# Score matmuls of the dot attention in two 128x64 tiles, and its softmax denominators dealt out anew

## What is computed

```python
# layer 0
x_l = (x @ W + b).reshape(N, 8, 64)
scores = alpha_l[:, None, :] * alpha_r[None, :, :]        # per head, N x N
att = softmax(where(adj > 0, scores, -9e15), axis=1)
x = layernorm(x + relu(einsum('ijh,jhc->ihc', att, x_l)))
# layer 1: "dot attention"
q = x (as 8 heads of 64) * 64 ** -0.5; k = x2; v
scores = einsum('hnd,hmd->hnm', q, k)                     # per head, N x N
attn = softmax(where(adj > 0, scores, -9e15), axis=-1)
x = layernorm(x + einsum('hnm,hmd->hnd', attn, v))
```

## Time and profile before

| | |
|---|---|
| median of 3 runs | 4104.07 us (4103.87 to 4105.66) |
| profiled execution, its own time | 4103.82 us |
| its span, first to last instruction | 4102.3 us |
| mean granted TensorE clock, share of 2.4 GHz | 0.950 |
| busy share of the span: PE, DVE, ACT, POOL | 94%, 76%, 62%, 37% |
| dot attention | from about 2009 to 3940 us |

### The profile page before, as it was taken

How to read it: one execution, slowest core, us unless ns; L and a number is a source line. 1 busy time by engine, 2 the same in 40 slices (tenths; PEclk the granted TensorE clock), 3 DMA queues, 4 the chain that set the end, 5 groups by cost and what they waited for, 6 DMA issues and landing times. The chain is left out here.

```text
span 4102.3 us, 55678 instructions
## 1 busy us (share of the span) xinstructions
PE 3871.6 (94%) x19385; PEld 1354.5 (33%) x19385; DVE 3128.7 (76%) x3078; ACT 2527.7 (62%) x2396; POOL 1525.1 (37%) x1115
## 2 busy tenths in 40 slices
PE   7887999999999999976699999999999999999987
PEld 5564222222222222235333333333333333333345
DVE  5555999999999999978677677676777676677656
ACT  3444888888888888842255555555555555555520
POOL 3332000000000000015467666666766666676620
PEclk9998999999999999975799999999999999999975
DMA  7875111111111111136699999999999999999864
GB/s 272 295 275 181 39 40 40 49 45 40 41 39 39 52 44 39 41 118 233 160 183 185 191 190 192 190 190 184 185 190 192 190 190 188 186 184 192 179 170 144
DMA packets 339912, 592.36 MB, mean 144 GB/s; under 512 B 29248, under 2 KB 201280, under 8 KB 339776
## 3 DMA queue, kind: packets, MB, share of 16 engines
q0 software_dynamic: 84224, 302.29, 37.5%
q1 hardware_dynamic: 238400, 262.89, 21.2%
q10 hardware_dynamic: 17152, 25.43, 1.8%
HBM read 262.70 MB, written 59.38 MB: 79 GB/s over the span
## 5 line engine op out<-in xcount | busy, mean ns | idle before, releaser
L1117 DVE TENSOR_TENSOR a_weights<-a_psS,maskT 128x1024 f32<-128x1024 f32 x1024 | 1205.6, 1219 | 582.1 <-ACT a_psS L1082 582.1
L1082 ACT ACTIVATE a_psS<-a_psS,a_shift 128x1024 f32<-128x1024 f32 x1024 | 1071.7, 1084 | 801.3 <-PE a_psS L1010 801.2
L477 ACT ACTIVATE g_weights<-al_bc,g_shift,g_xl 128x1024 f32<-128x1024 f32 x1024 | 1187.8, 1232 | 166.7 <-DVE g_total L523 80.4
L516 DVE TENSOR_TENSOR g_weights<-g_weights,maskT 128x1024 f32<-128x1024 f32 x1024 | 1175.6, 1218 | 97.5 <-ACT g_weights L477 96.6
L1010 PE MATMUL a_psS<-a_q,a_k 128*128 128x512 f16 x4096 | 974.5, 381 | 18.0 <-DMA a_k<-k_scratch 16.6
L1027 PE MATMUL a_psO<-a_weights,a_v 128*64 128x512 f32 x4096 | 988.0, 604 | 0.0
L568 PE MATMUL g_psO<-g_weights,g_xl 128*64 128x512 f32 x4096 | 965.9, 603 | 17.8 <-DVE g_weights L516 17.8
L1140 POOL TENSOR_TENSOR a_pool_total<-a_pool_total,a_weights 128x1024 f32<-128x1024 f32 x336 | 898.5, 2674 | 0.0
L1010 PEld LDWEIGHTS a_psS<-a_q,a_k 128*128 128x128 f16 x4096 | 358.7, 98 | 798.5 <-DVE a_weights L1117 312.5
L1148 POOL DMA_DIRECT2D a_dma_total<-a_weights x480 | 415.9, 867 | 523.7 <-DVE a_weights L1117 415.3
L599 POOL DMA_DIRECT2D o_scratch<-g_o x16 | 8.9, 559 | 1387.9 <-ACT g_d L486 1387.9
(11 more groups left out here) (135 smaller groups left out, 1846.9 us busy)
## 6 DMA issues: line engine op xcount, KB each, us to landing
a_dma_total<-a_weights POOLq DMA_DIRECT2D x512, 512.0 KB, 5.1
adj_sb<-in_adj_dram SPq DMA_DIRECT2D x128, 512.0 KB, 5.5
g_xl<-xl_scratch SPq DMA_DIRECT2D x128, 260.0 KB, 2.8
a_k<-k_scratch SPq DMA_DIRECT2D x256, 128.0 KB, 5.1
a_v<-in_L_gnn_v_dram SPq DMA_DIRECT2D x128, 256.0 KB, 3.1
al_bc<-alpha_scratch SPq DMA_DIRECT2D x16, 1024.0 KB, 4.9
f_oT<-o_scratch SPq DMA_DIRECT2D x16, 1024.0 KB
a_q<-q_scratch SPq DMA_DIRECT2D x64, 256.0 KB, 6.9
```

The lines of the kernel that those rows point to most:

```text
L477: nc.scalar.activation(w[:, u % NP, h, :], al_bc[:, par, h, :], ACT.Exp, bias=shift_bc[:, par, h:h + 1], scale=xl[:, slot, u % KB, 2 * C + ...
L516: nc.vector.tensor_tensor(w[:, u % NP, h, :], w[:, u % NP, h, :], maskT[:, ds(q * JB + u, 1), ds(ic * IC, IC)] .rearrange("p a c -> p (a c)"),
L1082: nc.scalar.activation(psS[n % RING][:], psS[n % RING][:], ACT.Exp, bias=shift_bc[:, g % 2, h:h + 1], scale=SCALE).then_inc(exped, 1)
L1117: nc.vector.tensor_tensor(w[:, u % NP, h, :], psS[n % RING][:].rearrange("p a c -> p (a c)"), maskT[:, j, (g // PAIRS) * IC:(g // PAIRS + ...
```

## The change

Three things are altered in `attend_dot`.

1. Each score matmul of 128 keys becomes two of 64 keys. The first has keys 0 to 63 of the tile as stationary operand (128x64) and writes partitions 0 to 63 of the same `psS` bank, the second has keys 64 to 127 and writes partitions 64 to 127. The moving operand of both is the same. A unit has 16 score matmuls instead of 8.
2. The elementwise sums are dealt out anew. Head 0: GpSimd adds all 32 tiles (31 additions in a group instead of 22). Head 1: VectorE takes tiles 2, 3, 7, 11, ... 31 (9 tiles, 8 additions, as many as it made for head 0 before), and transfers take the other 23, alternating between the two chains by their place among these (`dma_place`), not by `j`. The waits follow.
3. `denominators` has the same 8 calls in another order: two for head 0 (`pool_total`), then six for head 1 (both transfer totals, `dve_total`).

```diff
--- before.py
+++ after.py
@@ -928,18 +928,27 @@
 
         block = ctx.enter_context(nc.Block())
 
-        def by_pool(j):
-
-            return j == 1 or j >= 4 and j % 4 != 3
-
         def pool_adds_by(u):
 
             g, j = divmod(u, NT)
-            return g * sum(by_pool(t) for t in range(NT)) + sum(by_pool(t) for t in range(j + 1))
+            return g * (NT - 1) + j
+
+        def by_dve(j):
+
+            return j == 2 or j % 4 == 3
 
         def dve_adds_by(u):
 
             return (u + 1) // 4
+
+        def dma_place(j):
+
+            return sum(not by_dve(t) for t in range(j))
+
+        def dma_adds_by(u):
+
+            g, j = divmod(u, NT)
+            return g * len(range(dma_place(j) % 2, dma_place(NT), 2)) + dma_place(j) // 2 + 1
 
         @block.sync
         def _(sp):
@@ -1007,10 +1016,12 @@
                         pe.wait_ge(masked, n - RING + 1)
                     for hf in range(2):
                         for part in range(2):
-                            last = nc.tensor.matmul(psS[n % RING][:, hf, :],
-                                                    k_sb[:, slot, h, (u % KB) * P:(u % KB + 1) * P],
-                                                    q_sb[:, par, part, h, hf * HALF:(hf + 1) * HALF],
-                                                    start=(part == 0), stop=(part == 1))
+                            for low in (0, C):
+                                keys = (u % KB) * P + low
+                                last = nc.tensor.matmul(psS[n % RING][low:low + C, hf, :],
+                                                        k_sb[:, slot, h, keys:keys + C],
+                                                        q_sb[:, par, part, h, hf * HALF:(hf + 1) * HALF],
+                                                        start=(part == 0), stop=(part == 1))
                     last.then_inc(scored, 1)
 
             def values(u):
@@ -1033,16 +1044,16 @@
                 pe.wait_ge(o_taken, g + 1)
                 pe.wait_ge(pool_added, pool_adds_by((g + 1) * NT - 1))
                 pe.wait_ge(dve_added, dve_adds_by((g + 1) * NT - 1))
-                for chain in range(2):
-                    pe.wait_ge(dma_added[chain], 16 * (g + 1) * (NT // 2))
-                for step, totals in enumerate(((pool_total[:], dma_total[:, g % 2, 0, :]),
-                                               (dve_total[:], dma_total[:, g % 2, 1, :]))):
-                    for h in range(2):
-                        for hf in range(2):
-                            row = 32 * (2 * h + hf)
-                            last = nc.tensor.matmul(psO[row:row + 32, 0, :], onesF[:, 0:32],
-                                                    totals[h][:, hf * HALF:(hf + 1) * HALF],
-                                                    start=(step == 0), stop=(step == 1))
+                for j in (NT - 3, NT - 2):
+                    pe.wait_ge(dma_added[dma_place(j) % 2], 16 * dma_adds_by(g * NT + j))
+                for h, total, first, close in ((0, pool_total[:], True, True),
+                                               (1, dma_total[:, g % 2, 0, :], True, False),
+                                               (1, dma_total[:, g % 2, 1, :], False, False),
+                                               (1, dve_total[:], False, True)):
+                    for hf in range(2):
+                        row = 32 * (2 * h + hf)
+                        last = nc.tensor.matmul(psO[row:row + 32, 0, :], onesF[:, 0:32],
+                                                total[:, hf * HALF:(hf + 1) * HALF], start=first, stop=close)
                 last.then_inc(d_summed, 1)
 
             for u in range(GROUPS * NT):
@@ -1092,15 +1103,15 @@
         def _(dve):
             def add(u):
                 g, j = divmod(u, NT)
-                dve.wait_ge(masked, 2 * u + 1)
+                dve.wait_ge(masked, 2 * u + 2)
                 if j == 3:
                     if g > 0:
                         dve.wait_ge(d_summed, g)
-                    other = w[:, (u - 1) % NP, 0, :]
+                    other = w[:, (u - 1) % NP, 1, :]
                 else:
                     dve.wait_ge(dve_added, dve_adds_by(u - 1))
                     other = dve_total[:]
-                nc.vector.tensor_tensor(dve_total[:], other, w[:, u % NP, 0, :], ALU.add).then_inc(dve_added, 1)
+                nc.vector.tensor_tensor(dve_total[:], other, w[:, u % NP, 1, :], ALU.add).then_inc(dve_added, 1)
 
             def mask(u, h):
                 g, j = divmod(u, NT)
@@ -1111,9 +1122,10 @@
                     dve.wait_ge(w_used, freed + 1)
                     if h == 0:
                         dve.wait_ge(pool_added, pool_adds_by(freed + 1 if freed % NT == 0 else freed))
+                    elif by_dve(freed % NT):
                         dve.wait_ge(dve_added, dve_adds_by(freed + 1 if freed % NT == 2 else freed))
                     else:
-                        dve.wait_ge(dma_added[freed % 2], 16 * (freed // 2 + 1))
+                        dve.wait_ge(dma_added[dma_place(freed % NT) % 2], 16 * dma_adds_by(freed))
                 nc.vector.tensor_tensor(w[:, u % NP, h, :], psS[n % RING][:].rearrange("p a c -> p (a c)"),
                                         maskT[:, j, (g // PAIRS) * IC:(g // PAIRS + 1) * IC],
                                         ALU.mult).then_inc(masked, 1)
@@ -1141,22 +1153,23 @@
 
             def add_by_dma(u):
                 g, j = divmod(u, NT)
-                chain = u % 2
+                chain = dma_place(j) % 2
+                before = dma_adds_by(u) - 1
                 pool.wait_ge(masked, 2 * u + 2)
-                if j >= 2:
-                    pool.wait_ge(dma_added[chain], 16 * (u // 2))
+                if before > 0:
+                    pool.wait_ge(dma_added[chain], 16 * before)
+                if dma_place(j) >= 2:
                     pool.dma_start(dma_total[:, g % 2, chain, :], w[:, u % NP, 1, :], accum_op=ALU.add
                                    ).then_inc(dma_added[chain], 16)
                 else:
-                    if u >= 2:
-                        pool.wait_ge(dma_added[chain], 16 * (u // 2))
                     if g >= 2:
                         pool.wait_ge(d_summed, g - 1)
                     pool.dma_start(dma_total[:, g % 2, chain, :], w[:, u % NP, 1, :]).then_inc(dma_added[chain], 16)
 
             for u in range(GROUPS * NT):
-                add_by_dma(u)
-                if by_pool(u % NT):
+                if not by_dve(u % NT):
+                    add_by_dma(u)
+                if u % NT > 0:
                     add(u)
 
 
```

## The result

| | before | after |
|---|---|---|
| median | 4104.86 us (4103.87 to 4106.24, 4 runs) | 3990.85 us (3988.95 to 3992.29, 4 runs) |
| profiled execution, its own time | 4103.82 us | 3992.29 us |
| its span | 4102.3 us | 3990.8 us |
| mean granted TensorE clock | 0.950 | 0.948 |

The ratio is 0.9722, 95% interval 0.9705 to 0.9739: 2.8% faster, 114 us by the medians. The forecast was 3990 us, range 3983 to 4014.

A forecast was written before the change was run, and what follows sets the result against it. TensorE was taken to set the dot stage's time. Savings of 105.6 us in 15 groups, 7.7 in the first and 0.2 at the end sum to 113.5, from 4103.8 to 3990 us, range 3983 to 4014.

The forecast's parts named there:

- TensorE bounds, and only its stream counts: Dot stage: TensorE, busy for all of its 1790.00 us, sets the time, so only its stream's cost matters.
- 0.24 to 0.255 us of each period is the passage, paid for width: Dot stage: switching between scores and values costs 0.24 us per 3.70 us unit; equal widths bring 3.445, 0.255 less.
- the first spacing after a passage: Score block: the first gap between matmuls after a switch from values may be long, the others nearer to 0.216 us.
- Halves keep the price of the whole: Score block: 16 matmuls of 64 columns cost what 8 of 128 did, 0 extra; at the other bound 1.74 us more.
- The two rows taken as nearest: Trace evidence for the split scores: layer 0's 32-wide rounds, 0.054 us an instruction, and 128-column loads, at most 0.12 each.
- The middle case in R1: Score halves overlap only partly, as three tiles gave 2.38 times: 0.27 us a pair, time near 4220 us; no separate chance.
- R1: Score matmuls: the two halves do not stream together; fully apart about 4880 us; chance 0.09.
- Denominators 0.86 dearer a group: Group border: head 1's two tiles get three calls each, 6 rounds for 4, 2.58 us, 0.86 more on TensorE.
- A group 113.06 us: Dot stage: 32 units of 3.445 us plus 2.58 and 0.24 at the border make 113.06 us, 120.1 before.
- The verdict: GpSimd in the dot stage: its 31 additions, 93 us (bounds 81 and 105), stay covered in a group of 113.
- one term: GpSimd: an addition without a transfer was taken as 3.0 us from start to start, bounds 2.62 and 3.39.
- Fewer transfers bring nothing: Dot stage: nothing on TensorE waits for a transfer until the very end, where 1.1 us less wait nets 0.2 us.

The follow-up runs named there:

- split_only: The kernel before with only the score matmuls split into two halves of 64 keys, sums and denominators as before: 3977.24 us, ratio 0.9688.
- deal_only: The changed kernel with the score split undone, so new sums and denominator order with 128-wide scores: 4114.99 us, ratio 1.0026.
- one_tile: The changed kernel with both halves of every score matmul sent to one column tile, half of the scores left out: 4869.43 us.
- fold_chain: The changed kernel with VectorE adding one of the two transfer totals to its own, leaving head 1 four denominator calls instead of six: 3977.07 us.
- no_vector_adds: The changed kernel without VectorE's additions: GpSimd adds all 32 tiles of head 0, transfers take all 32 of head 1: 3978.26 us.
- head1_wide: The changed kernel with head 1's scores 128 wide again, head 0's still in two halves of 64: 4117.8 us.
- unit_apart: The changed kernel with a unit's score matmuls reordered: keys 0 to 63 of both heads, then keys 64 to 127 of both: 4052.62 us.
- halves_apart: The changed kernel with, for each head, the four score matmuls of keys 0 to 63 before the four of keys 64 to 127: 3991.67 us.

## Why the prediction was right, point by point

**TensorE bounds, and only its stream counts.** Right: `split_only`, `deal_only`, `one_tile`, `fold_chain` and `no_vector_adds` moved by what their streams of rounds and passages say (3978, 4117, 4870, 3977, 3977 expected; 3977, 4115, 4869, 3977, 3978 measured), although, between 2140 and 3780 us, GpSimd's load was between 0.55 and 0.89 of the stretch and the DMA share between 0.49 and 0.98 (`one_tile` the lowest, `no_vector_adds` the highest).

**0.24 to 0.255 us of each period is the passage, paid for width.** Right in size, 3.44 instead of 3.70. The trace of before already had the evidence in two places, each difference alone, and `head1_wide` confirms it with the kernel's own matmuls. What I had only guessed, that the first spacing after a passage is the long one, is right, but it is a small part for the scores: in the trace of before the first of the seven spacings is 0.226, the others 0.216; the values' first round is 0.05 longer than the others. The larger part, 0.10 and 0.09, lies between the last round of one kind and the first start of the next.

**Halves keep the price of the whole.** Right (16 records span 1.89); `one_tile` shows the 880 us that hung on it. The load of 64 columns takes 0.110 us (median), that of 128 columns took 0.098 before, so per column the loads did become slower, and they stay hidden. The two rows taken as nearest, the 32-wide rounds and the loads in a row, were good guides. The middle case in R1, from three tiles at 2.38 times (the Trainium skill, TensorE: Matmul & The Clock Gate, "Measured speedup vs the span model"), did not come true: two tiles gave the full two. Three tiles occur in no run here.

**Denominators 0.86 dearer a group.** Right: 2.72 for 1.85, and 12.1, 13.6 and 13.8 us by `deal_only`, `split_only` and `fold_chain`.

**A group 113.06 us.** Measured 113.02. In the profiled pair the dot stage, from its first scores to the last copy of denominators, is 1927.95 and 1813.87 us long, 114.1 less for 113.5 forecast. By parts: 8.1 up to the first denominators for 7.7, and 105.9 for 105.8 in the fifteen groups behind them and the end. It begins 2.5 us later than in the profile of before, for which nothing in the change speaks; in the profiles of the eleven kernels it begins anywhere from 2010.2 to 2015.1. So the mechanism and its terms are confirmed to about half a microsecond, but that the total came within 1 us of the median is partly luck.

**GpSimd.** The verdict was right, one term was mis-sized: an addition with no transfer issued beside it is 2.35 us long and starts 2.80 after the one ahead (2901.05 to 2903.85), not 3.0; the one right behind the issue of a transfer is 2.65. The prediction said that no such addition occurs before; the first additions of the 16 groups are of that kind there, and 2.35 us long (2346 to 2358 ns). The margin was a little larger than forecast. `no_vector_adds` shows the other end: with a transfer in every unit additions in the stretch read start 2.9 to 3.3 us apart, which still fits under 3.445.

**Fewer transfers bring nothing.** Right, and the runs go further than the text did: the new deal as a whole brings nothing either. I had costed its 0.86 us at the border without noting that the split with the old deal would be the faster kernel.

## What to carry to other kernels

Where TensorE alternates between matmuls whose stationary operands have different widths, compare a block between passages with the same block in a row: what is over (here 0.255 us in 3.70) comes back if all are cut to one width. Cutting is free when the pieces lie in different column tiles; that is shown here for two pieces of 64 columns, 16 bits, with 512 columns moving. Look at small reductions at a border in the same way: what counts is the longest queue on one tile, so deal the totals evenly, or let an engine with room fold them first. Before reordering matmuls that fill a buffer, follow the wait chain that starts when the buffer is complete: `unit_apart` kept TensorE's work and lost 62 us, most of them to that chain. A part of a change that relieves engines off the critical path should be tried without; here it cost 12 to 14 us.

## What the runs showed of the hardware

- A change of width costs 0.11 us from 64 to 128 columns and 0.09 back, and 0.05 more in the first 32-bit round behind it, whose loads then don't run ahead; a change of type at one width costs nothing that can be seen (scores to values 1.73, values to scores 1.71, what the rounds need by themselves).
- 16-bit matmuls of 64 columns in two column tiles stream fully at once, 16 in 8 rounds of 0.216 us, with a load for each; in one tile they take 16 rounds (`one_tile`, period 5.17).
- Matmuls of a free column tile start ahead of queued ones of a busy tile: past three of them in `halves_apart`, 31 ns behind the first of them, with the period unchanged. A greater distance was not measured.
- GpSimd's addition of 128x1024 takes 2.35 us with no transfer issued right before it (159 of 160 such additions in the changed kernel lie between 2.35 and 2.37), 2.65 behind the issue of one, and 2.62 to 3.07 where a transfer is issued in every unit.
